# Moving the first half's output products two steps later in attention, and the second norm's chunks with them

## The chip, the cores and the metric

The program runs on one core of one Trainium2 chip. The metric is the device time of one execution in microseconds. TensorE (PE) does matrix products and transposes, VectorE (DVE) and ScalarE (ACT) element-wise work, GpSimd (POOL) slower element-wise work, and SyncE (SP) only issues transfers. Each engine takes its own instructions strictly in the order in which they are written and waits on semaphores that the others raise.

## The reference, cut to what matters

Two transformer layers over x of 4 x 1024 x 512, f32. In each layer:

```python
h = norm(x) * (1 + scale) + shift
q, k, v = heads(h @ wq), heads(h @ wk), heads(h @ wv)      # 16 heads of 32; layer 0 turns q and k by position
attn = softmax(q @ k.T / sqrt(32))
x = x + gate * ((attn @ v) @ wo)                           # layer 0: no gate, a bias
h = norm(x) * (1 + scale2) + shift2
x = x + gate2 * (gelu(h @ w1 + b1) @ w2 + b2)
```

Layer 1 has 4 key and value heads for its 16 query heads. Products that need the precision are made from two f16 halves of each operand, so one product is three matmuls.

## The kernel before

The work is eight passes `i` = 0 to 7: batches 0 to 3 of layer 0, then batches 0 to 3 of layer 1. A pass is `attention(i)` and then `forward(i)` (the two feed-forward products, 32 chunks). The order is written out by hand for each engine.

**Attention** runs over 64 steps of eight blocks (a block is four of the 16 heads for one half of the queries: blocks 0 to 3 have tokens 0 to 511, blocks 4 to 7 the rest). A step `s` holds two units (`u` = 2s and 2s + 1) of two score products each. So PE makes four scores `w` = 4s to 4s + 3 into three PSUM banks (score `w` waits for exponential `w - 3`), and ACT takes four exponentials. Two steps later PE multiplies the probabilities with the values (`values`). Every second step it adds up the softmax sums with ones (`totals`). Before that, the sums of two units are added on another engine (`add_probs`, number `m`): on POOL for `m` < 56, on VectorE for the last eight, `m` = 56 to 63, which stand in VectorE's order at steps 57, 58, 59, 60, 61, 62, 63 and 63. `probs` has six slots: the exponential of unit `u` waits until the sum that reads unit `u - 6` is done. So unit 118 (step 59, first half) waits for `m` = 56, unit 119 (step 59, second half) for `m` = 57, unit 123 for `m` = 59 and unit 127 (the last) for `m` = 61. `sums` has three slots, so `add_probs(m)` also waits for a `totals`: `m` = 57 for that of step 58, 59 for that of step 60, 61 for that of step 62, 63 for that of step 63. The last `totals`, of `m` = 62 and 63, comes after everything else in attention, and only then PE starts `forward(i)`.

Beside this, steps up to 54 carry **maxima** (four more score products on PE and four reductions on VectorE in a step, for the next block; block 7 is the last, so steps 55 to 63 have none), at the end of step 54 a small transpose for block 7's row maxima, and **fills** between the scores of a step. The fills that matter here:

- `("wo", i, t)`, t = 0 to 3: `out_tile` on PE, 12 matmuls for 128 tokens; then `residual` on VectorE (adds to x, takes the norm's statistics; three instructions in layer 1, two in layer 0, whose bias POOL adds in `add_bias`). After tile 3 VectorE aggregates the statistics, POOL takes the root (`deviation("ln2", i, 0)`, in its order at `m` = 56 behind `add_probs` 55 and in layer 0 two `add_bias`), and VectorE, which stands in `norm_apply` until then, writes the normalised rows (four instructions, L1430).
- `("ln2", i, 0, c)`, c = 0 to 3, two per step: `norm_chunk`, four transposes on PE, one pass of ACT (high half, L1167, behind the third exponential of the step), two of VectorE (low half, L1453 and L1454). In a step VectorE does its fills ahead of its `add_probs`.

POOL's order after `deviation` is: `finish(5)` (which needs ACT's work of step 58), `normalise(6)`, and so on.

The lines that place these fills:

```python
for t in range(4):
    at[WO_AT + t] = [("wo", i, t)]
for t in range(2):
    at[LN2_AT + t] = [("ln2", i, 0, 2 * t), ("ln2", i, 0, 2 * t + 1)]
```

Of the kernel before, what the change touches and what calls it, by code (L numbers as in the profile page):

```python
# [38 lines left out]
L0_CHUNKS, L1_CHUNKS = 24, 21  # L39
MAX_AT = (4, 6, 8, 10, 12, 14, 16, 18, 20, 22, 24, 26, 28, 30, 32)  # L40
MAX_AT_K = (0, 2, 5, 7, 9, 11, 14, 16, 18, 20, 23, 25, 27, 29, 32)
WO_AT = 53
LN2_AT = 60
BIAS_AT = (49, 49, 50, 51, 53, 54, 56, 56)
TURNS = ((("k", 1, 0), -1, 1, 5), (("k", 1, 1), 3, 3, 10), (("q", 0, 1), 11, 13, 29), (("q", 1, 1), 25, 27, 57))

# [52 lines left out]
def fills_of(i):  # L99
# [12 lines left out]
# [4 lines that stand above are left out]
    return at  # L116
# [1681 lines left out]
```

## Time and profile before

| | |
|---|---|
| median of 3 runs | 3954.56 us (3951.26 to 3955.85) |
| the profiled execution | 3957.61 us, span 3955.8 us |
| PE busy | 3746.3 us, 95% of the span |
| VectorE busy | 2471.2 us, 62% |
| ACT, POOL busy | 1603.8 and 1613.5 us, 41% each |
| TensorE's granted clock, mean | 0.98 |

PE is busy nearly all the time, but an average over stages hides where it waits. The change acts on the last dozen steps of each of the eight attentions, so it is there that engines, waits and clock are to be read.

### The profile page before, as it was taken

The numbers are of one execution on the slowest core, as the hardware profiler recorded it, in microseconds if no ns is written. First come the engines' busy times: TensorE is split into PE (matmuls) and PEld (weight loads), VectorE is DVE, ScalarE is ACT, GpSimd is POOL, SyncE is SP. The second block draws the span as 40 slices with busy tenths as digits, with TensorE's granted clock in tenths as the row PEclk, the third lists the DMA queues.
The fourth block names the chain that finished last, engine by engine and source line by source line (L and its number), as shares of the span: only waits on it lengthen the run. The fifth ranks groups of instructions, "written<-read, shape, count | busy, mean of one in ns | idle before, by whom it ended". The sixth has DMA issues, their size and how long they took to land.

```text
span 3955.8 us, 76367 instructions
## 1 busy us (share of the span) xinstructions
PE 3746.3 (95%) x31828; PEld 1559.4 (39%) x31828; DVE 2471.2 (62%) x3951; ACT 1603.8 (41%) x2807; POOL 1613.5 (41%) x907
## 2 busy tenths in 40 slices
PE   7988999999998989999899999999999999999999
PEld 4422444333543335433354333433344333543344
DVE  5677735766457755467654777467664776467752
ACT  1466313554125642155521663136621563126621
POOL 2467212672216742066510672137520672126611
PEclk8899999999999999999999999999999999999999
DMA  5233243212423123431232112311123112311122
GB/s 153 48 99 119 85 107 81 72 55 84 109 76 87 41 91 91 106 75 53 100 101 83 34 42 89 115 44 29 65 96 98 31 40 81 114 54 26 63 67 96
DMA packets 139110, 306.67 MB, mean 78 GB/s; under 512 B 19680, under 2 KB 59636, under 8 KB 137872
## 3 DMA queue, kind: packets, MB, share of 16 engines
q10 hardware_dynamic: 50944, 174.62, 13.6%
q1 hardware_dynamic: 87824, 127.17, 12.1%
q8 instruction: 253, 4.15, 0.4%
q14 instruction: 89, 0.73, 0.1%
HBM read 223.46 MB, written 36.66 MB: 66 GB/s over the span
## 4 chain that ended last, share of the span: by engine, by line
PE 79%; DVE 7%; POOL 5%; issue 4%; ACT 3%; DMA 1%; ACTq 0%; SPq 0%; POOLq 0%; DVEq 0%
PE ps L931 15%; PE ps L834 12%; PE ps L835 12%; PE ps L836 12%; PE ps L1029 9%; PE ps L871 7%; PE ps L1044 5%; PE ps L888 3%; POOL sums L730 3%; ACT probs L1209 3%; DVE mcol L1532 2%; PE ps L947 2%; PE ps L852 1%; DVE ring L1582 1%; DVE turn L1466 1%
## 5 line engine op out<-in xcount | busy, mean ns | idle before, releaser
L1532 DVE TENSOR_REDUCE mcol<-ps 128x1 f32<-128x512 f32 x2048 | 1290.0, 683 | 441.2 <-PE ps L931 226.7
L730 POOL TENSOR_TENSOR sums<-probs 128x1024 f32<-128x1024 f32 x448 | 1065.2, 2392 | 943.0 <-PE ps L1044 510.9
L1209 ACT ACTIVATE probs<-ps 128x512 f32<-128x512 f32 x2048 | 1098.8, 608 | 812.0 <-PE ps L931 564.3
L931 PE MATMUL ps<-qs,ks 98*32 98x512 f16 x8192 | 800.6, 389 | 105.4 <-ACT probs L1209 93.5
L931 PE MATMUL ps<-ks,qs 97*32 97x512 f16 x7040 | 697.3, 385 | 53.7 <-DVE mcol L1532 41.5
L1355 ACT ACTIVATE sums<-ps,cols 128x512 f32<-128x512 f32 x256 | 175.8, 687 | 1097.0 <-PE ps L836 1097.0
L1029 PE MATMUL ps<-probs,v_sb 128*32 128x512 f32 x4096 | 548.5, 612 | 0.0
L931 PEld LDWEIGHTS ps<-qs,ks 98*32 98x32 f16 x8192 | 215.5, 97 | 589.9 <-ACT probs L1209 363.9
L834 PE MATMUL ps<-ring,probs 128*128 128x512 f16 x1024 | 388.0, 379 | 0.3 <-DVE probs L1627 0.3
L834 PE MATMUL ps<-aT,ring 128*128 128x512 f16 x1024 | 388.1, 379 | 0.0
L836 PE MATMUL ps<-aT,ring 128*128 128x512 f16 x1024 | 388.0, 379 | 0.0
L835 PE MATMUL ps<-aT,ring 128*128 128x512 f16 x1024 | 387.9, 379 | 0.0
L836 PE MATMUL ps<-ring,probs 128*128 128x512 f16 x1024 | 387.9, 379 | 0.0
L835 PE MATMUL ps<-ring,probs 128*128 128x512 f16 x1024 | 387.8, 379 | 0.0
L931 PEld LDWEIGHTS ps<-ks,qs 97*32 97x32 f16 x7040 | 188.4, 96 | 375.8 <-DVE mcol L1532 150.5
L1626 DVE CAST probs<-sums 128x512 f16<-128x512 f32 x256 | 132.7, 518 | 320.2 <-ACT sums L1355 320.2
L871 PE MATMUL ps<-hT,wqkv 128*128 128x512 f16 x1248 | 302.7, 388 | 8.8 <-DVE hT L1454 7.5
L1044 PE MATMUL ps<-sums,ones 128*32 128x512 f32 x2048 | 276.2, 615 | 1.0 <-DVE sums L1525 1.0
L715 POOL TENSOR_TENSOR turn<-turn 128x512 f32<-128x512 f32 x32 | 44.9, 1403 | 532.5 <-DVE turn L1466 532.5
L1627 DVE TENSOR_TENSOR probs<-sums,probs 128x512 f16<-128x512 f32 x256 | 203.7, 796 | 8.8
L1466 DVE SCALAR_TENSOR_TENSOR turn<-ps,bias,trig 128x512 f32<-128x512 f32 x128 | 90.2, 747 | 167.1 <-PE ps L871 167.1
L871 PEld LDWEIGHTS ps<-hT,wqkv 128*128 128x128 f16 x1248 | 115.9, 99 | 172.6 <-issue 33.5
(112 smaller groups left out, 3471.9 us busy)
## 6 DMA issues: line engine op xcount, KB each, us to landing
ring<-halves ACTq DMA_DIRECT2D x208, 512.0 KB, 3.3
qs<-hl SPq DMA_DIRECT2D x192, 128.0 KB, 4.1
ring<-halves SPq DMA_DIRECT2D x48, 512.0 KB, 6.2
ring<-in_weights ACTq DMA_DIRECT2D x39, 512.0 KB, 4.6
halves<-ring ACTq DMA_DIRECT2D x37, 512.0 KB, 2.9
ks<-hl SPq DMA_DIRECT2D x120, 128.0 KB, 4.4
dcopy<-inverses SPq DMA_DIRECT2D x56, 256.0 KB
probs<-in_x SPq DMA_DIRECT2D x8, 1024.0 KB, 8.3
```

Of the source, the lines that this page charges most:

```text
L730: pool.tensor_tensor(sums[:, m % SUM_SLOTS, :, :], prob(u - 2), prob(u), ALU.add).then_inc(sum_set[0].sem, 1)
L834: pe.matmul(dst, lhs[0], rhs[0], start=first, stop=False)
L835: pe.matmul(dst, lhs[0], rhs[1], start=False, stop=False)
L836: return pe.matmul(dst, lhs[1], rhs[0], start=False, stop=last)
L871: mm = pe.matmul(bank, qkv(lw, weight_at(kind, i, hh, part, c), P), hT[:, lx, c, tok], start=(q == 0), stop=(q == 11))
L931: mm = pe.matmul(bank[cut, :], lhs[:, cut], rhs, start=True, stop=True)
L1029: mm = pe.matmul(ps[32 * q:32 * q + 32, 4, :], values_of(i, hh)[:, kt, value_cut(i, hh, 4 * g + q)], prob(u + q // 2)[:, q % 2, :], start= ...
L1044: mm = pe.matmul(ps[32 * q:32 * q + 32, 5, :], ones32[:, :], sums[:, (m + q // 2) % SUM_SLOTS, q % 2, :], start=(m % 8 == 0), stop=(m % 8 ...
L1209: act.activation(prob(u)[:, e, :], ps[:, w % SCORE_BANKS, :], ACT.Exp).then_inc(exp_done.sem, 1)
L1355: act.activation(g32[:, n % 2, :], ps[:, 4 + n % 2, :], ACT.Gelu, bias=col[:, n % FC:n % FC + 1], scale=1 / WS).then_inc(gelu_done.sem, 1)
L1532: dve.tensor_reduce(mcol[:, blk % 2, 4 * j + qt, half:half + 1], src, AX.X, ALU.max).then_inc(n_free[0], 1)
L1627: dve.tensor_tensor(fT[:, n % 4, 1, :], g32[:, n % 2, :], fT[:, n % 4, 0, :], ALU.subtract).then_inc(f_set.sem, 1)
```

## The change

The output products of tokens 0 to 511 move from steps 53 to 56 to steps 55 to 58, and the second norm's chunks from steps 60 and 61 to 62 and 63, in all eight passes. What follows the last output product on VectorE (statistics, `norm_apply`) moves with it. No instruction is added or removed.

```diff
-WO_AT = 53
-LN2_AT = 60
+WO_AT = 55
+LN2_AT = 62
```

## Rows read from the trace of the kernel before

**Rows 1.** The page: the span, and the chain that ended last.
```profile
span 3955.8 us, 76367 instructions
...
PE 79%; DVE 7%; POOL 5%; issue 4%; ACT 3%; DMA 1%; ACTq 0%; SPq 0%; POOLq 0%; DVEq 0%
```

**Rows 2.** Windows of pass 5: steps 45-46; 53-54, 55-56, 57-58, 59 on; 57.
```profile
core 0: us, PE busy (x) PEld busy (x) DVE busy (x) ACT busy (x) POOL busy (x), PEclk, DMA share, GB/s
2786.03:2792.77 6.74, 6.67 (x94) 2.16 (x89) 5.27 (x10) 4.13 (x8) 4.88 (x3) 1.00 0.11 40
2812.32:2826.44 14.12, 12.07 (x114) 4.21 (x106) 9.60 (x15) 4.45 (x8) 5.73 (x3) 1.00 0.05 19
2826.44:2836.38 9.94, 9.94 (x83) 3.58 (x85) 5.33 (x7) 4.34 (x8) 4.90 (x3) 1.00 0.72 264
2836.38:2843.27 6.89, 5.04 (x60) 1.48 (x56) 3.40 (x11) 5.15 (x10) 3.54 (x3) 1.00 0.21 83
2843.27:2866.28 23.01, 19.12 (x189) 6.15 (x181) 15.77 (x17) 14.24 (x27) 2.43 (x2) 0.93 0.04 13
...
2836.38:2838.56 2.18, 1.91 (x28) 0.58 (x24) 0.52 (x6) 1.08 (x2) 1.82 (x1) 1.00 0.62 254
```

**Rows 3.** Windows of pass 1 (layer 0): steps 53-54, 55-56, 57-58, 59 on.
```profile
882.94:895.57 12.63, 12.03 (x114) 4.30 (x106) 7.82 (x13) 4.24 (x8) 9.41 (x6) 1.00 0.06 23
895.57:905.50 9.93, 9.93 (x81) 3.58 (x84) 3.48 (x10) 4.34 (x8) 8.03 (x5) 1.00 0.75 254
905.50:912.41 6.91, 5.05 (x62) 1.48 (x57) 0.44 (x1) 5.15 (x10) 5.99 (x5) 1.00 0.24 96
912.41:939.78 27.37, 20.24 (x189) 7.00 (x181) 18.89 (x21) 15.07 (x28) 2.43 (x2) 0.88 0.03 12
```

**Rows 4.** Windows ahead of and in two stretches at the lower clock.
```profile
912.44:915.85 3.41, 0.79 (x16) 0.18 (x8) 3.41 (x6) 0.76 (x2) 1.15 (x1) 1.00 0.00 0
915.85:922.68 6.83, 6.04 (x40) 2.74 (x44) 2.38 (x3) 4.01 (x8) 0.00 (x0) 0.50 0.01 4
2854.62:2858.03 3.41, 1.61 (x20) 0.59 (x24) 2.33 (x4) 3.41 (x8) 0.00 (x0) 1.00 0.17 55
2858.03:2861.44 3.41, 3.41 (x28) 0.71 (x16) 2.52 (x3) 1.06 (x3) 1.27 (x1) 0.50 0.08 27
```

**Rows 5.** Timeline of POOL, pass 1: sum 55 and the root.
```profile
start us, us, engine line op out<-in xcount [idle before <-releaser]
905.87 2.36 POOL L730 TENSOR_TENSOR sums<-probs 128x1024 f32<-128x1024 f32 x1 [2.27 <-PE ps L1044]
...
910.92 1.02 POOL L710 TENSOR_TENSOR rs<-sd,eps 128x4 f32<-128x4 f32 x1
```

**Rows 6.** Timeline of VectorE, passes 1 and 5.
```profile
904.98 0.35 DVE L1420 BATCH_NORM_AGGREGATE mv<-stats 128x2 f32<-128x6 f32 x4
911.97 2.77 DVE L1430 TENSOR_SCALAR v_sb<-ks,mv,rs 128x512 f32<-128x512 f32 x4 [6.64 <-POOL rs L710]
...
2836.58 0.36 DVE L1420 BATCH_NORM_AGGREGATE mv<-stats 128x2 f32<-128x6 f32 x4
2840.39 1.92 DVE L1430 TENSOR_SCALAR v_sb<-ks,mv,rs 128x512 f32<-128x512 f32 x4 [3.45 <-POOL rs L710]
...
2849.63 0.81 DVE L1453 TENSOR_SCALAR turn<-ps,ab 128x512 f32<-128x512 f32 x1 [2.84 <-ACT aT L1167]
...
2851.92 0.69 DVE L1454 TENSOR_TENSOR aT<-turn,aT 128x512 f16<-128x512 f32 x1
...
2863.89 1.22 DVE L1525 TENSOR_TENSOR sums<-probs 128x1024 f32<-128x1024 f32 x1 [0.57 <-PE ps L1044]
```

**Rows 7.** Timeline of ACT, passes 1 and 5: exponentials and what they waited for.
```profile
888.61 2.06 ACT L1209 ACTIVATE probs<-ps 128x512 f32<-128x512 f32 x4 [2.47 <-POOL sums L730]
...
915.99 0.60 ACT L1209 ACTIVATE probs<-ps 128x512 f32<-128x512 f32 x1 [2.76 <-DVE sums L1525]
...
2848.23 0.60 ACT L1209 ACTIVATE probs<-ps 128x512 f32<-128x512 f32 x1 [0.39 <-PE ps L931]
...
2854.26 0.60 ACT L1209 ACTIVATE probs<-ps 128x512 f32<-128x512 f32 x1 [2.64 <-DVE sums L1525]
```

**Rows 8.** Timeline of PE, pass 5: the last totals, ahead of the feed-forward.
```profile
2865.29 1.04 PE L1044 MATMUL ps<-sums,ones 128*32 128x512 f32 x8
```

## The prediction

> **What bounds the kernel now.** I read first the page's chain of work that ended last: 79% of the span is PE's, 7% VectorE's, 5% POOL's [rows 1]. So PE sets the time, except where another engine keeps it waiting, and those places have to be looked for stretch by stretch. For that I cut two passes into windows at the first score of a step: pass 5 of layer 1 [rows 2] and pass 1 of layer 0 [rows 3]. Two steps with maxima and no output product take 6.74 us, with PE busy for 6.67. Steps 53 and 54, which carry maxima and two output products, take 14.12 in layer 1, with PE idle for 2.05 of them: VectorE stands in front of its reductions waiting for an output product, and PE then waits for the reductions' banks. Steps 55 and 56, with output products and no maxima, take 9.94, all of it PE. Steps 57 and 58, with neither, take 6.89 and PE is idle for 1.85: the second half of step 57 waits for POOL's sum 55. From step 59 to the first feed-forward product it is 23.01 in layer 1 and 27.37 in layer 0. In layer 0 PE is idle there for 7.1 us, and the reader should see why in three views. VectorE has its statistics at 905.33, but the root comes at 911.94, because POOL first makes sum 55 and two bias additions [rows 5, 6]. VectorE idles 6.64 us in `norm_apply` and its sum 56 is late, so the exponential of step 59 waits until 915.99 [rows 7]. PE, busy for 0.79 of 3.41 us, is then granted half its clock for 6.83 us [rows 4].
>
> **The change part by part.** Nothing is added, so every term is a length of a stretch that gets or loses something. Call the first feed-forward product F.
>
> *Steps 53 and 54 lose two output products.* Layer 1: they become like the two regular steps, which also hold a transpose for row maxima at their end: 6.74 for 14.12, **-7.4 us** per pass [rows 2]. Layer 0 gets less, since POOL is late there with its sums (bias additions stand between them): the second half of step 53 waits for POOL until 888.61, which is 5.67 after the stretch begins at 882.94 [rows 3, 7]. From there come four exponentials 0.49 apart (2.06 for the row of four), then values, totals and the transpose of step 54, about 1 us each for the first two by [rows 8], less for the third: 5.67 + 1.7 + 2.4 = 9.8 for 12.63, **-2.8**. The bounds are 12.63 (no gain) and 5.67 + 2.06 = 7.7 (-4.9); I keep 9.8 because the regular steps also show a tail of about that size after their last score.
>
> *Steps 55 and 56* keep their 9.94: the same two tiles' worth of products, with tiles 0 and 1 in place of 2 and 3. POOL's sums are needed later than PE reaches them.
>
> *Steps 57 and 58 gain two output products.* They become like 55 and 56, and the wait for POOL's sum 55 goes, since its unit's scores now come behind an output product: 9.94 for 6.89, **+3.05** per pass; in layer 0 9.93 for 6.91, the same [rows 2, 3]. Of the 5.2 us of products that arrive, some 2 are covered by the idle time of PE that was there.
>
> *Step 59 to 61: the new wait.* Let S be the first score of step 59. Behind the fourth output product, VectorE ends its statistics where it did relative to step 57: 0.56 after it in layer 1 (2836.94 against 2836.38), 0.17 ahead of it in layer 0 (905.33 against 905.50) [rows 2, 3, 6]. POOL has nothing to do by then (its sums and bias additions end before), so the root takes only its own time, 1.02 and 0.4 for the small addition ahead of it, an estimate: S + 1.96 and S + 1.23. `norm_apply` then takes 1.92 or 2.77; the two passes show one each [rows 6]. I take 2.77, for the reason that in pass 1 a pass of POOL over an f32 tile fell into it, and after the change POOL's `finish(5)` stands right behind the root. Queued behind `norm_apply` on VectorE is sum 57 (1.2 by the row of sum 63 [rows 6]), and for that waits the exponential of unit 119 in step 59. It comes at about S + 5.9 in layer 1 and S + 5.2 in layer 0, where it could come at about S + 2.5. PE has sent its free banks' scores and idles for 2.3 to 2.9. Three more scores follow the exponentials at 0.49, then values and totals, 2 us: step 61 begins 3.5 later, at S + 9.4 and S + 8.7. Step 61 has no totals and no fill: 2.2, by the last of [rows 2].
>
> On the 2.77 a page has a rule. The Trainium skill, page "SBUF — State Buffer", section "Who interferes with whom", says that a tensor_scalar in a two-port mode and a GpSimd instruction exclude each other, and that whoever starts first keeps the ports for its whole instruction. By it, `norm_apply` starting first would stay at 1.92 and POOL would wait, 0.85 less per pass.
>
> *Step 62 on: the chunks now lie in front of the last sums.* Let U be the start of step 62. The third exponential came 2.78 after the start of step 60 in pass 5 (2848.23 against 2843.27 + 2.18), with 0.6 of waits in it, so U + 2.2. ACT's high halves follow, and VectorE's low halves begin 1.4 after that exponential and take 3.0 for two chunks (2849.63 to 2852.61) [rows 6, 7]: U + 6.6. Only then comes sum 61: U + 7.8. The exponential of unit 127, the third of step 63, waits for it, as that of step 61 did for sum 59 before the change (2.64 us [rows 7]). Behind it stand the last two chunks: low halves from U + 9.2 to U + 12.2, then sums 62 and 63, 2.4, to U + 14.6, and the last totals and F 1.0 later (2865.29 to 2866.28 [rows 2, 8]): U + 15.7. Before, this chain ran behind PE's steps 62 and 63; now nothing is left for PE to do beside it, and it idles for some 3.4 us ahead of the last totals.
>
> From S to F this makes 9.4 + 2.2 + 15.7 = 27.3 in layer 1, for 23.0: **+4.3**. In layer 0 8.7 + 2.2 + 15.7 = 26.6 for 27.4: **-0.8**.
>
> *The sum without the clock.* Layer 1: -7.4 + 3.05 + 4.3 = 0.0. Layer 0: -2.8 + 3.05 - 0.8 = -0.6. Four passes each: -2.4 us.
>
> *The clock.* Both idle times are of the kind after which the trace shows half clock (1.2 for 2.4 GHz): PE busy for 0.79 of 3.41, then 6.83 at 0.50; busy for 1.61 of 3.41, then 3.41 at 0.50 [rows 4]. The rows of before (one such stretch per pass at least) are already in the 27.37 and 23.01, while my chain above has none. A stretch of 3.41 costs 1.7 where PE alone counts, nothing where VectorE does. Near step 60 I take 1.2; the one caused by the idle end falls into the feed-forward, which is all PE: 1.5. That is 2.7 for eight passes, 21.6; since the stretches will not lie equally in all, I take 17. The Trainium skill, page "TensorE: Matmul & The Clock Gate", section "HAM oscillation — how this bites in real kernels", prices the loss as the throttled time times one half, so 1.7 for each 3.41 with no discount; by it eight passes with two such stretches would lose 27.
>
> Sum: -2.4 + 17 = +15 on the profiled execution's 3957.61, which is 3972.6. That execution was 3.05 above the median of the runs, so the median should be about **3970**.
>
> **The rivals.** *Forecast, chance 0.45:* the gain of steps 53 and 54 is spent on the two new waits, and the clock adds to it; 3960 to 3985, 3970 likeliest.
>
> *The clock falls no oftener than before, chance 0.25.* For it: layer 0 has its stretch of 6.83 already, and the new idle times there are shorter than the 3.41 of the old one. Then it is the sum without the clock with little on top: 3954.6 - 2.4 = 3952, up to 3958.
>
> *Faster, chance 0.20.* The point that decides is when VectorE is free behind `norm_apply` and behind the chunks. If `norm_apply` stays at 1.92 (0.85 less) and the low halves and sums 61 to 63 pack 1.2 closer (sum 61 no longer holds back unit 127), each pass gains 2: 8 x 2.05 = 16.4, with -2.4 makes -19, so 3936, and with part of it 3945. For it: layer 1 really has 7.4 us per pass to give back and the chain of the end is my construction, not a row. Against it: sum 61 and the chunks stand in that order on VectorE.
>
> *Slower than forecast, chance 0.10.* If both stretches at half clock are 6.83 long, as in pass 1, the clock costs 2.6 more per pass at the most: 3970 + 21 = 3991.
>
> That the change does nothing of what it says can't be; that it does nothing for the time is the second case.
>
> **How the numbers follow.** The likeliest case gives 3970. For 8 in 10 the range goes down into the faster case to 3940 and up into the last one to 3986. A measurement of this kernel can tell about 0.2% (7.9 us) from no change; slower by more than that is 0.45 + 0.10 = 0.55, within it 0.25, faster 0.20. The forecast's own range is 3960 to 3985.
>
> **What the profile after would show.** Steps 53 and 54 at 6.7 us in layer 1 and near 9.8 in layer 0; 55 to 58 at 19.9; VectorE's wait in `norm_apply` at 1.4 for 6.64 and 3.45; an exponential of step 59 that waits for VectorE's sum for about 3 us in all eight passes; sum 63 ending some 3.4 us after PE's last values; and stretches at half clock that begin near F. I am wrong if PE is not idle ahead of F, if step 59 and 60 take under 8 us in layer 1, or if the granted clock in the feed-forward stays at 1.00.

## The result, and the profile after

The changed kernel takes 3974.53 us (median of 4 runs, 3971.03 to 3979.92) where the kernel before takes 3954.82 (4 runs): a ratio of 1.0049, 95% interval 1.0036 to 1.0062. It is slower by 20 us; 3970 was forecast. The profiled spans are 3971.6 and 3955.8 us.

The same windows as in [rows 2] and [rows 3], each cut at the first score of its step, show what became of the stretches. Pass 5 of the changed kernel: steps 45-46; 53-54, 55-56, 57-58, 59 on.

```profile
core 0: us, PE busy (x) PEld busy (x) DVE busy (x) ACT busy (x) POOL busy (x), PEclk, DMA share, GB/s
2793.68:2800.44 6.76, 6.68 (x94) 2.17 (x90) 5.28 (x10) 4.13 (x8) 4.89 (x3) 1.00 0.11 40
2819.90:2826.43 6.53, 6.46 (x91) 2.05 (x83) 5.15 (x9) 4.13 (x8) 4.72 (x2) 1.00 0.11 41
2826.43:2836.36 9.93, 9.93 (x81) 3.58 (x84) 4.85 (x7) 4.34 (x8) 6.36 (x3) 1.00 0.74 270
2836.36:2846.29 9.93, 9.93 (x84) 3.56 (x80) 5.28 (x8) 5.44 (x10) 2.36 (x1) 1.00 0.13 51
2846.29:2876.42 30.13, 21.33 (x188) 6.22 (x181) 17.68 (x26) 14.22 (x26) 4.18 (x4) 0.82 0.04 13
```

And pass 1, steps 57-58 and 59 on:

```profile
899.73:909.66 9.93, 9.93 (x84) 3.56 (x80) 4.70 (x10) 5.44 (x10) 4.91 (x4) 1.00 0.18 71
909.66:938.18 28.52, 19.98 (x188) 6.09 (x180) 17.17 (x20) 14.81 (x27) 3.78 (x4) 0.92 0.04 13
```

Steps 53 and 54 are regular steps now, 6.53 for 14.12, and 57 and 58 are full of output products. The last stretch has grown from 23.01 to 30.13 in pass 5 and from 27.37 to 28.52 in pass 1. PE is idle there for 8.8 and 8.5 us.

Where it idles, the timeline shows. First pass 5 in steps 58 to 60: VectorE around `norm_apply` (L1430), POOL's root and `finish(5)` (L768), the exponential that waits, and PE behind it:

```profile
2846.49 0.36 DVE L1420 BATCH_NORM_AGGREGATE mv<-stats 128x2 f32<-128x6 f32 x4
...
2846.93 0.20 POOL L708 TENSOR_TENSOR sd<-mv,eps 128x4 f32<-128x4 f32 x1 [7.85 <-DVE mv L1420]
...
2848.20 1.16 POOL L768 TENSOR_TENSOR aT<-ocopy,aT 128x512 f16<-128x512 f32 x1
2848.27 2.74 DVE L1430 TENSOR_SCALAR v_sb<-ks,mv,rs 128x512 f32<-128x512 f32 x4 [1.42 <-POOL rs L710]
2850.93 2.35 DVE L1525 TENSOR_TENSOR sums<-probs 128x1024 f32<-128x1024 f32 x2
...
2852.26 3.04 ACT L1209 ACTIVATE probs<-ps 128x512 f32<-128x512 f32 x6 [3.95 <-DVE sums L1525]
...
2852.91 1.59 PE L931 MATMUL ps<-qs,ks 98*32 98x512 f16 x12 [4.05 <-ACT probs L1209]
```

The wait for the root is down from 3.45 to 1.42 us (6.64 before in layer 0 [rows 6], 1.42 now as well), but sum 57 is the one behind it, and ACT and PE stand for 4 us. Then the end of the attention: VectorE's last chunks and sums, PE's last `totals` (L1044) and the first feed-forward product (L834):

```profile
2869.15 0.81 DVE L1453 TENSOR_SCALAR turn<-ps,ab 128x512 f32<-128x512 f32 x1 [1.49 <-ACT aT L1167]
...
2872.05 2.35 DVE L1525 TENSOR_TENSOR sums<-probs 128x1024 f32<-128x1024 f32 x2
...
2874.55 1.94 PE L1044 MATMUL ps<-sums,ones 128*32 128x512 f32 x8 [3.23 <-DVE sums L1525]
2876.42 0.61 PE L834 MATMUL ps<-aT,ring 128*128 128x512 f16 x1
```

The 1.94 us for matmuls that took 1.04 in [rows 8] are at the lower clock. Two more windows of this kernel show it: the one ahead of the fall, and the 6.83 us at half clock, which reach into the feed-forward.

```profile
2869.25:2872.66 3.41, 1.55 (x16) 0.16 (x8) 3.34 (x5) 1.55 (x3) 0.00 (x0) 1.00 0.00 0
2872.66:2879.49 6.83, 4.94 (x16) 1.38 (x17) 1.75 (x2) 1.88 (x2) 0.00 (x0) 0.50 0.50 177
```

The whole account, worked out by cutting all eight passes at the first scores of steps 53, 55, 57, 59, 61 and 63, at the first feed-forward product F, and 44 groups of three matmuls behind F (sums over the eight passes, us). These 44 groups, called the first chunks below, are the first products of six feed-forward chunks and the second ones of five; at full clock they take 28.5 us.

| stretch | before | after | difference |
|---|---|---|---|
| steps 0 to 52 | 1691.7 | 1685.6 | -6.1 |
| 53, 54 | 106.7 | 65.7 | -41.0 |
| 55, 56 | 79.5 | 79.5 | 0.0 |
| 57, 58 | 58.2 | 79.4 | +21.2 |
| 59, 60 | 73.2 | 86.7 | +13.4 |
| 61, 62 | 78.1 | 48.2 | -29.9 |
| 63 to F | 49.6 | 98.3 | +48.8 |
| the first chunks, from F | 227.9 | 237.3 | +9.4 |
| all the rest | 1590.9 | 1590.9 | 0.0 |

### The profile page after: what moved, and what is told of

Read it like the earlier page. It is cut to its first block, busy times and chain, and to the rows that moved or that the text cites. A ratio compares the mean times of both kernels' runs of the same rounds, so it can differ in the third digit from the quotient of the medians.

```text
span 3971.6 us, 76367 instructions
## 1 busy us (share of the span) xinstructions
PE 3748.4 (94%) x31828; PEld 1555.5 (39%) x31828; DVE 2470.0 (62%) x3951; ACT 1603.4 (40%) x2807; POOL 1616.8 (41%) x907
## 4 chain that ended last, share of the span: by engine, by line
PE 79%; DVE 7%; POOL 5%; issue 5%; ACT 3%; DMA 1%; ACTq 0%; SPq 0%; POOLq 0%; DVEq 0%
PE ps L931 15%; PE ps L834 12%; PE ps L835 12%; PE ps L836 12%; PE ps L1029 9%; PE ps L871 7%; PE ps L1044 5%; PE ps L888 3%; ACT probs L1209 2%; POOL sums L730 2%; DVE mcol L1532 2%; PE ps L947 2%; PE ps L852 1%; DVE ring L1582 1%; DVE sums L1525 1%
## 5 line engine op out<-in xcount | busy, mean ns | idle before, releaser
L834 PE MATMUL ps<-aT,ring 128*128 128x512 f16 x1024 | 392.1, 383 | 0.0
L834 PE MATMUL ps<-ring,probs 128*128 128x512 f16 x1024 | 388.0, 379 | 0.3 <-DVE probs L1627 0.3
L1044 PE MATMUL ps<-sums,ones 128*32 128x512 f32 x2048 | 279.9, 623 | 30.3 <-DVE sums L1525 30.3
```

The costliest lines, as they stand in the source:

```text
L834: pe.matmul(dst, lhs[0], rhs[0], start=first, stop=False)
L1044: mm = pe.matmul(ps[32 * q:32 * q + 32, 5, :], ones32[:, :], sums[:, (m + q // 2) % SUM_SLOTS, q % 2, :], start=(m % 8 == 0), stop=(m % 8 ...
```

## The experiments

Theory: the 41 us of steps 53 and 54 are spent on products in 57 and 58, on a first wait (sum 57 behind `norm_apply`, step 59), on a second wait (the last sums behind the chunks' low halves, ahead of F) and on the clock behind both. Rivals: only one of the two waits is real; the late sums are the shadow of something else; the feed-forward's loss is not the clock's. The stretches below are sums over eight passes, in the order of the table above; each ratio is to runs of the kernel before that were taken together with that kernel's.

| kernel | 53-54 | 57-58 | 59-60 | 61-62 | 63 to F | first chunks | median us | ratio to before (95%) |
|---|---|---|---|---|---|---|---|---|
| before | 106.7 | 58.2 | 73.2 | 78.1 | 49.6 | 227.9 | 3954.8 | |
| after | 65.7 | 79.4 | 86.7 | 48.2 | 98.3 | 237.3 | 3974.5 | 1.0049 (1.0036 to 1.0062) |
| wo_only | 67.1 | 79.4 | 97.6 | 73.2 | 47.7 | 227.9 | 3953.3 | 0.9999 (0.9990 to 1.0008) |
| ln2_only | 106.7 | 57.3 | 62.4 | 47.2 | 98.3 | 236.4 | 3972.2 | 1.0045 (1.0033 to 1.0058) |
| sum_first | 64.0 | 79.4 | 44.6 | 51.9 | 102.5 | 240.3 | 3943.4 | 0.9970 (0.9958 to 0.9982) |
| fill_tail | 65.4 | 79.4 | 86.5 | 47.4 | 93.9 | 228.0 | 3967.7 | 1.0035 (1.0023 to 1.0048) |
| finish_first | 67.2 | 79.4 | 89.8 | 48.2 | 99.5 | 236.7 | 3983.4 | one run |
| old_places_root | 106.8 | 56.8 | 62.5 | 79.6 | 49.0 | 227.9 | 3944.2 | 0.9973 (0.9963 to 0.9983) |
| sums_ahead | 65.5 | 79.4 | 44.6 | 52.0 | 92.4 | 228.0 | 3924.4 | 0.9927 (0.9913 to 0.9940) |
| first_61 | 65.3 | 79.4 | 44.6 | 67.8 | 61.8 | 227.9 | 3911.3 | 0.9895 (0.9881 to 0.9908) |
| first_60 | 63.9 | 79.4 | 68.4 | 82.0 | 48.3 | 227.9 | 3928.8 | 0.9942 (0.9928 to 0.9955) |
| ahead_61 | 63.9 | 79.4 | 44.6 | 66.5 | 63.6 | 228.0 | 3907.9 | 0.9883 (0.9870 to 0.9897) |

Steps 0 to 52, which no kernel changes, give 1685.6 to 1696.8 us from one profile to another. So stretches tell more of a cause than the whole span of one profile does: up to 11 us of such a span can come from these steps.

### Each half of the change alone: wo_only and ln2_only

Both edits are against the changed kernel. wo_only:

```diff
-LN2_AT = 62
+LN2_AT = 60
```

> Output products at steps 55 to 58 as in the changed kernel, the norm's chunks back at steps 60 and 61. My theory (two waits, one behind norm_apply in step 59 and one behind the chunks ahead of the feed-forward): the first stays (steps 59 and 60 at 11 us or more, since the chunks of step 60 now lie in them), the second goes: the stretch from step 63 to the feed-forward falls from 12.3 back to about 6.5, and the first feed-forward chunks lose no clock. From step 59 on all eight passes look like layer 0 of before, 27.4 us: 4 x 0 and 4 x 4.3 = 17 against before, with -41 in steps 53-54 and +21 in 57-58: about 3952, within 8 us of before. Rival (the place of the chunks makes nothing, the wait behind norm_apply is the whole loss): as the changed kernel, 3974.

3953.31 us, no difference from the kernel before. Pass 5 from step 59: steps 59-60, 61-62, 63 to F, and the first chunks; then the exponential of step 59 that waits for VectorE's sum.

```profile
2835.09:2848.11 13.02, 8.71 (x68) 3.29 (x64) 7.39 (x15) 6.06 (x11) 2.35 (x3) 0.74 0.00 1
2848.11:2856.84 8.73, 7.08 (x68) 2.38 (x64) 6.64 (x9) 5.45 (x10) 0.84 (x1) 0.87 0.10 33
2856.84:2862.84 6.00, 6.00 (x60) 1.54 (x53) 3.79 (x3) 2.77 (x5) 0.63 (x1) 0.90 0.00 0
2862.84:2891.33 28.49, 28.49 (x137) 12.91 (x134) 19.18 (x31) 5.96 (x8) 5.68 (x5) 1.00 0.33 112
```

```profile
2841.05 2.06 ACT L1209 ACTIVATE probs<-ps 128x512 f32<-128x512 f32 x4 [3.94 <-DVE sums L1525]
```

The first wait is there with the chunks in their old place (from step 59 on the eight passes take 17.7 us more than before; 17 was expected), the second is gone, and so is the loss in the feed-forward. The rival with one wait only, 3974, is out.

ln2_only:

```diff
-WO_AT = 55
+WO_AT = 53
```

> Output products back at steps 53 to 56, the norm's chunks at steps 62 and 63. My theory: the end is paid in full (from step 63 on 12.3 for 6.2 us, +49, and 9 of clock in the feed-forward), while steps 59 to 62 lose the chunks and their waits (about 5.5 per pass, -44): +14, 3969. Rival (the end's wait is only the shadow of the late norm_apply): with norm_apply early as in before, the last sums are early too and the stretch from step 63 stays under 8 us: 3925 to 3935.

3972.23 us. Pass 5, step 63 to F and the first chunks, then the same two of pass 1:

```profile
2864.14:2875.83 11.69, 7.21 (x68) 2.15 (x61) 8.92 (x11) 4.70 (x9) 0.00 (x0) 1.00 0.00 1
2875.83:2904.33 28.50, 28.50 (x136) 12.94 (x133) 19.18 (x31) 5.96 (x8) 5.68 (x5) 1.00 0.33 112
...
929.31:941.03 11.72, 7.24 (x68) 2.15 (x61) 8.93 (x11) 4.70 (x9) 0.23 (x1) 1.00 0.02 3
941.03:971.15 30.12, 30.12 (x136) 13.32 (x134) 17.21 (x28) 7.29 (x10) 5.33 (x5) 0.95 0.32 106
```

With `norm_apply` in its old place the end still takes 11.7, so it is no shadow of the first wait: the chunks' late place alone makes it, and alone it costs nearly the whole 20 us. The price of the clock varies by pass: after the same idle end, nothing in pass 5 and 1.6 us in pass 1.

### The first wait taken away by order: sum_first

```diff
@@ VectorE, attention
                     for key in FILLS[i].get(s, ()):
                         if not by_scalar(key):
                             narrow(key)
-                        if key == ("wo", i, 3):
-                            norm_apply("ln2", i, 0)
...
                             add_probs(i, m)
+                    if ("wo", i, 3) in FILLS[i].get(s, ()):
+                        norm_apply("ln2", i, 0)
```

> The changed kernel with one thing turned round on VectorE: in step 58 sum 57 stands ahead of norm_apply and not behind it. My theory: the exponential of step 59 no longer waits, steps 59 and 60 fall from 10.8 to about 5.5 us and keep their clock, the end stays as it is: 3974.5 - 37 = 3937, which is below the kernel before. Rival (PE and ACT have no room there, the wait only moves to sum 58 or 59, which then stand behind norm_apply): steps 59 to 62 keep at least 14 us of their 16.9, 3955 or more.

3943.44 us. VectorE of pass 5 in steps 58 to 60, and steps 59-60 as a window:

```profile
2829.16 1.18 DVE L1525 TENSOR_TENSOR sums<-probs 128x1024 f32<-128x1024 f32 x1
2831.54 2.75 DVE L1430 TENSOR_SCALAR v_sb<-ks,mv,rs 128x512 f32<-128x512 f32 x4 [1.20 <-POOL rs L710]
```

```profile
2828.67:2834.16 5.49, 5.04 (x60) 1.39 (x56) 4.26 (x11) 4.51 (x9) 3.25 (x3) 1.00 0.01 1
```

Steps 59 and 60 fall by 42 us in eight passes, to 5.5 or 5.65 each, at full clock. Step 61 gives 3.8 back where sum 58 now is late (1.90 us, in layer 1 only), and the end and the chunks behind it 7 more, of which a lower clock in more passes is part. The kernel is 10 us below the one before and 31 below the changed one; 37 was expected.

### The clock by itself: fill_tail

```diff
@@ PE, attention
                         if s == totals_step(i, pair):
+                            if pair == SUMS // 2 - 1:
+                                for _ in range(14):
+                                    pe.matmul(ps[:, 0, :], wo[:, 0, 0, 0:P], wo[:, 0, 0, 512:1024], start=True, stop=True)
                             totals(i, 2 * pair)
```

> The changed kernel with 14 matmuls of no use (128x512, f16, into a score bank that is free by then) on PE ahead of the last totals, where PE is idle. It computes nothing else. My theory: 3 us of idle time are filled, no stretch at half clock begins there, the first feed-forward chunks go from 29.7 back to 28.5 us per pass (-9), and nothing else moves, since the last totals wait for sum 63 as before: 3965. Rival (the feed-forward's extra 9 us come from transfers or from VectorE and not from the clock): 3974 or more.

3967.73 us. The idle time of pass 5 with the matmuls of no use in it, then step 63 to F and the first chunks:

```profile
2870.21 3.19 PE L1073 MATMUL ps<-wo 128*128 128x512 f16 x14
2873.51 1.07 PE L1044 MATMUL ps<-sums,ones 128*32 128x512 f32 x8
```

```profile
2862.81:2874.51 11.70, 10.35 (x83) 3.45 (x75) 8.93 (x11) 4.70 (x9) 0.00 (x0) 1.00 0.00 0
2874.51:2903.01 28.50, 28.50 (x137) 12.91 (x134) 19.19 (x31) 5.96 (x8) 5.68 (x5) 1.00 0.33 112
```

More work, less time (each of the five runs is below each of the changed kernel's four): the first chunks are back at 28.50 us in all eight passes (-9.3), and the stretch to F loses 4.4 us, since the last `totals` run at full clock again. So the feed-forward's loss is the clock's. These two stretches give 14 us and the medians only 7; steps 0 to 52 took 11 us more in this profile than in the changed kernel's, so the size is best read from the stretches. What is left of the end, 11.7 us for 6.2 a pass, is the wait for sum 63 and costs 44 us in eight passes.

### What norm_apply's 2.75 us are: finish_first

```diff
@@ POOL, attention
-                    if m == 56:
-                        deviation("ln2", i, 0)
...
                         finish(i, m // 8 - 2)
+                    if m == 57:
+                        deviation("ln2", i, 0)
```

> The changed kernel with POOL's finish(5) ahead of the root of the second norm and not behind it. A look at norm_apply's time: my theory of the price 2.77 (an operation of POOL that runs beside it holds it up) gives 1.92 us in all eight passes, with the root about 0.5 us later in layer 1 and 1 us later in layer 0, so the exponential of step 59 comes within 0.4 us of where it was and the time is 3971 to 3976. If norm_apply stays at 2.7, its length has another cause, for instance the transfers of the weights in these steps.

One run, 3983.35 us, 7 above what was expected. Of the 10 us by which this profile is longer than the changed kernel's, 4.3 lie in steps 0 to 52 and 3.1 in steps 59 and 60. What the run is for shows at VectorE, pass 5:

```profile
2859.41 1.92 DVE L1430 TENSOR_SCALAR v_sb<-ks,mv,rs 128x512 f32<-128x512 f32 x4 [1.96 <-POOL rs L710]
```

With `finish(5)` out of its way `norm_apply` takes 1.91 or 1.92 us in all eight passes, for 2.74 or 2.75, and the later root takes the gain back: the wait is 1.96 for 1.42 here, and 3.44 in layer 0, where the root comes 2 us later and I had expected 1. Transfers are out as the cause.

### Was the old place bound by the same orders: old_places_root

The kernel before, with two orders changed:

```diff
@@ POOL, attention
+                    if m == 56:
+                        deviation("ln2", i, 0)
                     for tt, at_ in enumerate(BIAS_AT):
                         if layer(i) == 0 and m == at_:
                             add_bias(i, tt)
-                    if m == 56:
-                        deviation("ln2", i, 0)
@@ VectorE, attention
-                        if key == ("wo", i, 3):
-                            norm_apply("ln2", i, 0)
...
+                    if ("wo", i, 3) in FILLS[i].get(s - 1, ()):
+                        norm_apply("ln2", i, 0)
```

> The kernel before, places of all fills as in it, with two orders changed: POOL takes the root ahead of the two bias additions of step 56, and VectorE makes sum 56 ahead of norm_apply. My theory: layer 0's wait of 6.6 us in norm_apply was POOL's order; the exponential of step 59 comes some 3 to 4 us earlier there and the half clock behind it goes, layer 1 stays: 4 x -5 = -20, so 3934. Rival (in layer 0 POOL's sum 55 and the products bind just as much): at most 5 us less than before, 3948.

3944.19 us: half of what was expected. Layer 0, pass 1, VectorE's sum 56, POOL, and `norm_apply` (step 59 begins at 908.11 in this kernel):

```profile
902.77 2.24 DVE L1525 TENSOR_TENSOR sums<-probs 128x1024 f32<-128x1024 f32 x1 [1.73 <-ACT probs L1209]
...
903.89 1.18 POOL L708 TENSOR_TENSOR sd<-mv,eps 128x4 f32<-128x4 f32 x1
905.15 1.02 POOL L710 TENSOR_TENSOR rs<-sd,eps 128x4 f32<-128x4 f32 x1
906.14 2.71 POOL L738 TENSOR_TENSOR ks<-ks,row_bc 128x512 f32<-128x512 f32 x2
...
906.20 4.71 DVE L1430 TENSOR_SCALAR v_sb<-ks,mv,rs 128x512 f32<-128x512 f32 x4 [1.19 <-POOL rs L710]
```

Counted from the start of step 59 (912.41 in the kernel before), sum 56 is done 3.1 us ahead of it, where it was 3.4 behind, and `norm_apply` starts 1.5 us earlier than in [rows 6]. But POOL's two bias additions, moved behind the root, and `finish(5)` now lie beside it, so it takes 4.71 us for 2.77 and ends 0.5 us later than it did, with sum 57 behind it. Steps 59 and 60 of layer 0 take 8.2 to 9.9 us for 11.9; in layer 1 they stay, as expected.

### The end shortened in two ways: sums_ahead and first_61

sums_ahead is sum_first with VectorE's low halves of steps 62 and 63 behind the sums of these steps:

```diff
@@ VectorE, attention
-                        if not by_scalar(key):
+                        if not by_scalar(key) and key[0] != "ln2":
                             narrow(key)
...
                     if ("wo", i, 3) in FILLS[i].get(s, ()):
                         norm_apply("ln2", i, 0)
+                    for key in FILLS[i].get(s, ()):
+                        if key[0] == "ln2":
+                            norm_lo(key)
```

> As sum_first with chunks at steps 62 and 63, but in these two steps VectorE makes its sums 61, 62 and 63 ahead of the chunks' low halves. My theory of the order (unit 127 waits for sum 61, and sums 62 and 63 wait behind the low halves): the first wait goes, but now the feed-forward waits for the last low halves themselves, which end some 2 us earlier than sum 63 did: the stretch from step 63 falls from 12.8 to 10.5, about -17: 3926. Rival (what counts is the total of VectorE's work behind the last exponentials, in any order): 12 us or more in that stretch, 3940.

3924.43 us. The stretch from step 63 is 11.0 us in layer 0 and 12.1 in layer 1, a gain of 10 us and not 18; and 12 come from the feed-forward, which keeps its clock in all eight passes. The sum came out as expected, its parts did not. In pass 5 VectorE has sum 63 done at 2838.6 and then the last low halves:

```profile
2837.38 1.23 DVE L1525 TENSOR_TENSOR sums<-probs 128x1024 f32<-128x1024 f32 x1 [2.12 <-PE ps L1044]
...
2840.81 0.69 DVE L1454 TENSOR_TENSOR aT<-turn,aT 128x512 f16<-128x512 f32 x1
```

The low half ends at 2841.50 and F begins at 2841.55: F now waits for the chunks themselves.

first_61 is sum_first with `LN2_AT = 61`.

> Output products at steps 55 to 58, sum 57 ahead of norm_apply on VectorE as in sum_first, and the norm's chunks at steps 61 and 62 in place of 62 and 63. My theory: each step that the chunks lie further from the end takes part of their 3 us on VectorE off the way to the last sums: the stretch from step 63 falls from 12.8 to about 8 us (-38), the feed-forward's first chunks keep their clock (-12), steps 61 and 62 get 3 us longer (+25): about 3919. Rival (the end is paid wherever the chunks stand behind norm_apply, because ACT and VectorE need the same time for them): 3940 or more, as sum_first.

3911.31 us, 63 below the changed kernel and 43 below the kernel before. Pass 5, steps 59-60, 61-62, 63 to F, the first chunks:

```profile
2808.37:2813.86 5.49, 5.04 (x62) 1.40 (x57) 4.26 (x11) 4.51 (x9) 3.25 (x3) 1.00 0.01 1
2813.86:2822.57 8.71, 7.13 (x76) 3.08 (x72) 7.12 (x10) 6.19 (x11) 0.83 (x1) 1.00 0.09 33
2822.57:2831.89 9.32, 7.46 (x60) 1.81 (x53) 6.28 (x7) 3.37 (x7) 0.86 (x1) 0.82 0.00 0
2831.89:2860.38 28.49, 28.49 (x137) 12.89 (x134) 19.20 (x31) 5.96 (x8) 5.68 (x5) 1.00 0.33 112
```

Against sum_first, one step earlier is worth 41 us at the end and 12 of clock in the first chunks, for 16 in steps 61 and 62. Pass 5 has a stretch at half clock in its end, hence its 9.32 us; six of the other passes take 7.7 to 7.8 there and pass 4 takes 6.0.

### Where it turns: first_60 and ahead_61

first_60 is sum_first with `LN2_AT = 60`.

> As first_61, with the chunks one step earlier still, at steps 60 and 61. My theory gives a best place: the transposes of step 60 now reach PE about 2.7 us after the start of step 59, and norm_apply, behind sum 57, ends only near 5, so PE stands in front of them for about 2 us in each pass; the stretch from step 63 gets to its floor of about 6. Steps 59 and 60: 5.6 to 9.3, from step 63: 7.7 to 6.0, together +12: 3923. Rival (the earlier the chunks the better, since only the end counts): 3900 or less.

3928.81 us. The transposes of step 60 in pass 5:

```profile
2825.18 1.09 PE L852 MATMUL ps<-ident,v_sb 128*128 128x128 f32 x8 [2.70 <-DVE v_sb L1430]
```

PE stands in front of `norm_apply` for 2.70 us, as expected (2 were), and steps 59 and 60 grow by 24 us in all against first_61. Steps 61 and 62 grow by another 14, which was not expected: in six of the eight passes a stretch at half clock begins in them. The end is back at 6.0 us a pass (6.2 in the kernel before). So "the earlier the better" is out, and step 61 is the best of the three places in this order.

ahead_61 is sums_ahead with `LN2_AT = 61`.

> first_61 and sums_ahead together: chunks at steps 61 and 62, and VectorE's sums of these steps ahead of the low halves. If the two gains are the same gain (VectorE's low halves out of the way to the last sums), little is left of the second: sum 60 and 61 come 1 to 3 us earlier, the stretch from step 63 goes from 7.7 to 6.5: 3902 to 3908. If they add up in full (-19 as between sum_first and sums_ahead), it is 3892; if the order delays the transposes, whose banks VectorE frees, 3915 or more.

3907.93 us, the fastest here, 1.2% below the kernel before. Against first_61 the intervals overlap, so whether the second order adds anything at this place isn't settled; that it doesn't add its full 19 us is.

## Why the prediction was right

- *Steps 53 and 54.* Forecast -7.4 and -2.8 a pass, -40.8 in all; measured -7.6 and -2.6, -41.0 in all. In layer 0 9.3 to 9.6 us in three passes, as worked out from POOL (9.8); pass 1 took 11.2, with a stretch at half clock in it.
- *Steps 55 and 56.* Unchanged, as forecast.
- *Steps 57 and 58.* Forecast 9.94 for 6.9, measured 9.93. The sum is 21.2 and not 24.4, because passes 6 and 7 had taken 8.6 and 8.25 before, with a stretch at half clock that I had not read from the trace.
- *The wait behind norm_apply.* The exponential was put at S + 5.9 in layer 1 and came at S + 5.97 (2852.26 against 2846.29). In pass 1 it came 5.25 behind S, for 5.2. The 2.77 for `norm_apply` was right (2.74), and finish_first shows its reason. The Trainium skill, page "SBUF — State Buffer", section "Who interferes with whom", has the rule; the trace agrees with it, down to who starts first: POOL's `finish(5)` starts 0.07 us ahead of `norm_apply` (2848.20 and 2848.27), and `norm_apply` is the one that grows by 0.83. The 0.85 of the faster rival was therefore not to be had. Nor would starting first have kept `norm_apply` at 1.92, as the prediction has it: in pass 1 of the kernel before, its first instruction started 1.34 us ahead of `finish(5)`, and its fourth, which started 0.04 us behind `finish(5)`, took 1.39 for 0.54. It is four instructions, and POOL came in between two of them.
- *The length of that wait for PE.* Put at 2.3 to 2.9 us, it was 4.05 in pass 5. The chain took the exponentials right, but PE was out of work at S + 2.6, earlier than the chain had it, and then waited for the end of the exponential, 0.65 us after its start. That alone does not move the end; what it changes is the clock, which fell for 6.83 us in three of the four passes of layer 1 where I had priced one of 3.41. Steps 59 and 60 of layer 1 took 11.4 in these three passes and not 9.4 + 1.2. From S to F layer 1 lost 6.6 us a pass where 4.3 + 1.2 was forecast, layer 0 1.5 where it was -0.8 + 1.2. This is the term that was mis-sized, by some 9 us in all, and the time came out 5 above the forecast.
- *The end.* With U at the start of step 62, the last low half was put at U + 12.2 and ended at U + 12.0, sum 63 at U + 14.6 and ended at U + 14.3 (2874.4 against 2860.14), F at U + 15.7 (its own terms give 15.6) and came at U + 16.3, with the last `totals` at half clock. ln2_only shows that this end comes from the chunks' place alone, first_61 that most of it goes with another place (41 us of the 53 that sum_first has more there than the kernel before), sums_ahead that another order takes away only 10.
- *The clock in the feed-forward.* Forecast 12 us, measured 9.4; fill_tail takes it away. In pass 5 the stretch at half clock reaches 3.07 us beyond F (to 2879.49), and the first chunks take 1.51 longer (30.00 for 28.49): one half. That is the price that the Trainium skill, page "TensorE: Matmul & The Clock Gate", section "HAM oscillation — how this bites in real kernels", gives for throttled time, and this trace agrees where PE alone counts. It is not the price of the whole stretch: of the 6.83 us, 3.76 lay ahead of F, and for the first half of these PE only waited for VectorE.
- *The rivals.* "The clock falls no oftener" failed on the feed-forward, which had lost nothing in any pass before. The faster case failed on the port and on the order of sums and chunks, both of which held.

The sum was helped by an accident. The stretches that the change touches grew by 21.9 us where +15 was forecast, with 17 set for the clock and not the 21.6 of its own terms. Steps 0 to 52, in which nothing changed, took 6.1 us less in this profile than in that of before, so the two profiles lie only 15.8 apart. The medians lie 19.7 apart.

## What to carry to other kernels

When a piece of work is moved off a crowded stretch, read its followers on the slower engines too: here the products were worth moving, and what followed them in VectorE's order (a normalisation ahead of a sum, low halves ahead of the last sums) took back all of it and more. Where an engine makes both something urgent and something that is due later, put the urgent one first in its order, and then look for the place of the other from both ends: too late and it stands in front of the end, too early and its own input isn't there. Idle times of PE can also lower its clock, here those of 3.2 and 4.05 us, and then part of the price is paid in the next dense stretch.

## What was not expected of the hardware

- PE was busy for 1.55 of 3.41 us and the stretch at half clock began right after, while in ln2_only the same idle end left pass 5 at full clock throughout. So its length alone does not decide; what does is not shown here.
- 14 matmuls of no use made the kernel faster: 3967.7 for 3974.5 us.
- An operation of VectorE that normally takes 1.92 us for four took 2.75 beside one operation of POOL and 4.71 beside three. Work moved out of an engine's way in POOL's order can land beside it.
- POOL's addition of 128x4 numbers took 1.18 us in old_places_root and 0.20 in the changed kernel; the first stood beside VectorE's sum of two 128x1024 tiles.
